# Two-layer feed-forward of a macaron block: the two K halves of the first layer joined in PSUM, all eight groups of the second layer split into high and low parts

## The reference

```
x = x + 0.5 * ffn(layernorm(x))          # ffn: h = LN(x)*gamma + beta; silu(h @ w1 + b1) @ w2 + b2
x = x + attn(layernorm(x))               # sigmoid / tanh gates, a scan over time, output matmul
x = x + 0.5 * ffn(layernorm(x))
w = (q - 128) * scales[k // 128]         # one scale for 128 rows of K and one output column
```

## Time and profile before

| | |
|---|---|
| median of three runs | 780.07 us |
| the profiled execution | 778.86 us |
| its span, first to last instruction | 777.0 us |
| mean granted TensorE clock | 0.985 |
| busy: TensorE, ScalarE, VectorE, GpSimd | 95%, 85%, 82%, 82% of the span |
| first feed-forward, first product of tiles 0, 1, 2, 3 | 15.60, 40.10, 62.33, 82.15 us |
| second feed-forward, first product of tiles 0 and 2 | 462.43, 508.98 us |

### The profile page before, as it was taken

The page is one execution under the profiler, slowest core; times in us unless marked ns, Lnnn a source line. Parts: engine busy times, 40 slices in busy tenths (PEclk is TensorE's granted clock), DMA queues, the critical chain, the costliest instruction groups (busy, mean ns, idle before and its releaser), DMA issues.

```text
span 777.0 us, 14017 instructions
## 1 busy us (share of the span) xinstructions
PE 736.8 (95%) x3262; PEld 549.8 (71%) x3262; DVE 640.0 (82%) x1242; ACT 663.8 (85%) x1123; POOL 636.8 (82%) x821
## 2 busy tenths in 40 slices
PE   5698999999999999999999996989999999999996
PEld 4366777777777776668788783667777777777774
DVE  5377989999999998878778864779899999999886
ACT  5877999999999998778888887779989999999984
POOL 6588999999999987848666676889999999999853
PEclk7989999999999999999999999899999999999999
DMA  8640000000000000000000000000000110000001
GB/s 258 194 135 1 2 0 0 0 0 0 0 0 0 2 0 1 1 1 0 0 0 0 1 1 1 0 29 28 28 27 27 34 48 27 27 27 28 28 28 56
DMA packets 19820, 20.24 MB, mean 26 GB/s; under 512 B 1548, under 2 KB 19394, under 8 KB 19778
## 3 DMA queue, kind: packets, MB, share of 16 engines
q1 hardware_dynamic: 19680, 19.74, 7.8%
q10 hardware_dynamic: 98, 0.02, 0.0%
HBM read 11.37 MB, written 8.39 MB: 25 GB/s over the span
## 4 chain that ended last, share of the span: by engine, by line
PE 84%; issue 5%; POOL 5%; ACT 2%; DVE 2%; DMA 1%; ACTq 0%; DVEq 0%; POOLq 0%
PE ps_fc L867 28%; PE ps_z L867 26%; PE ps_z L901 13%; PE ps_fc L967 7%; PE ps_tr L860 4%; PE ps_tr L917 3%; POOL h_lo L393 2%; PE ps_fc L975 2%; POOL g_lo L403 1%; PE ps_fc L961 1%; DVE z_acc L685 1%; PE ps_z L860 1%; DMA rows<-in_L_attn_bc 1%; POOL xhat L372 1%; ACT xhat L532 0%
## 5 line engine op out<-in xcount | busy, mean ns | idle before, releaser
L685 DVE SCALAR_TENSOR_TENSOR z_acc<-ps_z,cols,z_acc 128x512 f32<-128x512 f32 x384 | 276.7, 742 | 25.2 <-PE ps_z L867 23.7
L403 POOL TENSOR_TENSOR g_lo<-g_full,g_hi 128x512 fp32r<-128x512 f32 x192 | 248.5, 1295 | 49.9 <-ACT g_hi L569 47.5
L547 ACT ACTIVATE u_sb<-ps_fc,cols 128x512 f32<-128x512 f32 x256 | 199.6, 780 | 60.8 <-PE ps_fc L867 54.9
L867 PE MATMUL ps_fc<-h_hi,q_sb 128*128 128x512 f32 x512 | 227.0, 443 | 6.1 <-DVE y_sb L674 3.9
L674 DVE SCALAR_TENSOR_TENSOR y_sb<-ps_fc,cols,u_sb 128x512 f32<-128x512 f32 x256 | 190.3, 743 | 50.5 <-ACT u_sb L547 50.4
L867 PE MATMUL ps_fc<-h_lo,q_sb 128*128 128x512 f32 x512 | 202.9, 396 | 0.0
L867 PE MATMUL ps_z<-g_hi,q_sb 128*128 128x512 f32 x384 | 155.2, 404 | 12.0 <-DVE z_acc L685 11.9
L867 PE MATMUL ps_z<-g_lo,q_sb 128*128 128x512 f32 x384 | 152.3, 397 | 0.0
L567 ACT ACTIVATE g_full<-y_sb 128x512 f32<-128x512 f32 x192 | 120.0, 625 | 9.8 <-DVE y_sb L674 9.8
L867 PEld LDWEIGHTS ps_fc<-h_hi,q_sb 128*128 128x128 f32 x512 | 97.7, 191 | 33.4 <-DVE y_sb L674 7.1
L901 PE MATMUL ps_z<-g_native,w_full 128*128 128x512 f32 x256 | 120.1, 591 | 0.0
(11 more groups left out here) (99 smaller groups left out, 980.5 us busy)
## 6 DMA issues: line engine op xcount, KB each, us to landing
resid<-in_L_attn_x SPq DMA_DIRECT2D x15, 512.0 KB, 4.4
out_x<-resid SPq DMA_DIRECT2D x15, 512.0 KB, 2.9
q_int<-in_L_ffn_fc_q SPq DMA_DIRECT2D x4, 512.0 KB, 7.0
resid<-in_L_attn_x SPq DMA_DIRECT2D x2, 256.0 KB, 3.0
out_x<-resid SPq DMA_DIRECT2D x2, 256.0 KB, 2.3
z_acc<-in_L_ffn_fc_scales SPq DMA_DIRECT2D x1, 256.0 KB, 9.2
wd_sb<-in_L_attn_Wd SPq DMA_DIRECT2D x1, 256.0 KB
wy_raw<-in_L_attn_Wy SPq DMA_DIRECT2D x2, 64.0 KB
```

What stands on the lines that cost most here:

```text
L403: nc.gpsimd.tensor_tensor(g_lo[:, slot, :], g_full[:, g % 2, :], g_hi[:, slot, :].bitcast(F32), ALU.subtract).then_inc(g_ready, 1)
L547: nc.scalar.activation(u_sb[:, f % 2, :], ps_fc1[:, f % 2, 0, :], ACT.Identity, bias=col(R_B1 + f), scale=col(R_S1 + f)).then_inc(u_ready, 1)
L685: nc.vector.scalar_tensor_tensor(out=z, in0=bank_of(g, n, par), scalar=col(R_S2 + KC * g + n), in1=z, op0=ALU.mult, op1=ALU.add).then_inc( ...
L867: last = nc.tensor.matmul(out, w, v, start=start and i == 0, stop=stop and i == len(pairs) - 1)
```

## The change

- First layer: each group has one bank of four, not two. `half_products` computes K half 0 in step f; then one instruction scales the bank in place by s1[0]/s1[1] and adds a bias (`scale_half`: on ScalarE in steps 0, 1, 5, 6, 7, on VectorE in steps 2, 3, 4); in step f + 1 `add_products` accumulates K half 1 on top. The silus read PSUM and take s1[1] as their scale. `u_sb` and `y_sb` are gone.
- beta leaves the tiles: its product with w1 is folded into the bias by small operations at the start. ScalarE now writes `h_hi` from `ps_tr` in one instruction (`round_h`), and VectorE writes `h_lo` from `ps_tr` (`lower_h`). It is `lower_h` that now signals `turned_out`. `h_full` and GpSimd's `h_low` are gone.
- Second layer: all eight groups are split. ScalarE's first sum takes group 0 (steps 4 and 5); VectorE adds seven groups, 14 additions for a tile where there were 12.
- The tables: `add_ffn` moves to steps 6 and 7, the variance to step 6, `lower_h` stands in steps 2 and 4, `round_h` in 1 and 3. The 14 warm-up matmuls go.

```diff
-    NATIVE = 2
-    RSQRT_AT = (5, 3, 2)
-    NORMALISE_AT = ((6, 7), (6, 7), (5, 6))
-    TURN_AT = ((4, 5), (2, 4), (0, 2))
-    ADD_AT = (5, 6)
+    SCALED_ON_ACT = (0, 1, 5, 6, 7)
+    SCALED_ON_DVE = (2, 3, 4)
+    VARIANCE_AT = 6
+    RSQRT_AT = (5, 2, 2)
+    NORMALISE_AT = ((6, 7), (5, 6), (5, 6))
+    TURN_AT = ((3, 5), (1, 3), (0, 2))
+    TURN_OUT_AT = ((4, 6), (2, 4), (1, 3))
+    H_LOWER_AT = ((5, 7), (3, 5), (2, 4))
+    FIRST_SUM_AT = (4, 5)
+    ADD_AT = (6, 7)
...
+            def scale_half(ff, f):
+                act.wait_ge(half_done, FC * ff + (f + 1))
+                nc.scalar.activation(bank, bank, ACT.Identity, bias=bias[:, f:f + 1],
+                                     scale=ratio[:, f:f + 1]).then_inc(scaled_on_act, 1)
...
+            def lower_h(ln, ff, par, c, bank=ps_tr):
+                dve.wait_ge(h_hi_ready, 2 * ff + (c + 1))
+                nc.vector.scalar_tensor_tensor(out=h_lo[:, par, c, :], in0=bank[:, :], scalar=col(R_GAMMA + c),
+                                               in1=h_hi[:, par, c, :].bitcast(F32), op0=ALU.mult,
+                                               op1=ALU.subtract).then_inc(turned_out, 1)
...
                     for f in range(FC):                      # VectorE
+                        if f in SCALED_ON_DVE:
+                            scale_half(ff, f)
                         if before or here:
-                            add_group(*group, range(1))
-                        second_group(FC * ff + f, f)
-                        if before or here:
-                            add_group(*group, range(1, KC))
+                            add_group(ff if here else ff - 1, (f - LAG) % FC, par if here else 1 - par)
+                        if behind and f in H_LOWER_AT[before]:
+                            lower_h(ln + 1, ff + 1, 1 - par, H_LOWER_AT[before].index(f))
...
                     for f in range(FC):                      # TensorE
-                        fc1(FC * ff + f, ff, f, par)
+                        half_products(ff, ln, f, par)
-                            fc2(ff, f - LAG, par)
+                            fc2(*group, 0)
+                            add_products(ff, ln, f - 1, par)
+                            fc2(*group, 1)
```

More of the change, by code:

```diff
@@ L195, in macaron_kernel @@
         fc2_done = sem("fc2_done")
+        z_begun = [sem(f"z{n}_begun") for n in range(KC)]
         z_added = [sem(f"z{n}_added") for n in range(KC)]
@@ L444, in tile @@
                             rsqrt(ln0 + 1, True)
[L445 to L449, removed]
+                        if not before and f == 1:
+                            normalise(ln0 + 1, 1, halves[0])
+                        if ff0 == 0 and not behind and f in XN_LOWER_AT:
+                            xn_low(0, 0, XN_LOWER_AT.index(f))
+                        if behind >= 1 and f == RESIDUAL_AT[before]:
+                            residual(ln + 1, t + 1)
                         if behind >= 2 or ff0 == 0:
@@ L475, in mixer_tile @@
                     rsqrt(t + (NT + 2), behind == 1)
[L476 to L480, removed]
+                for c in range(KC) if behind else ():
+                    xn_low(t + 1, 1 - par, c)
                 if behind == 1:
@@ L833, in mixer_tile @@
                         add_mixer(t - 1, 1 - par, half)
+                for c in range(KC) if not behind else ():
+                    lower_h(2 * NT, NT, 0, c, (ps_tr, ps_tr2)[c])
                 dve.wait_ge(state_ready, t + 1)
@@ L866, in products, with half_products @@
                 for i, (w, v) in enumerate(pairs):
-                    last = nc.tensor.matmul(out, w, v, start=start and i == 0, stop=stop and i == len(pairs) - 1)
+                    last = nc.tensor.matmul(out, w, v, start=start and i == 0, stop=stop and i == len(pairs) - 1,
+                                            skip_group_check=not start)
                 return last
-            def fc1(step, ff, f, par):
+            def half_products(ff, ln, f, par):
                 if f == 0:
-                    pe.wait_ge(h_ready, 2 * ff + 2)
-                wait(pe, y_ready, step - 1)
-                for k in range(KC):
-                    if type(ff) is int and ff == 0 and f == 0:
-                        pe.wait_ge(q1_ready, k + 1)
-                    last = products(ps_fc1[:, f % 2, k, :],
-                                    [(w[:, k, f * P:(f + 1) * P], h[:, par, k, :])
-                                     for w in q1_parts for h in (h_hi, h_lo)])
-                last.then_inc(fc1_done, 1)
@@ L883, in fc2, with add_products @@
-            def fc2(ff, g, par):
-                if native(g):
+                    pe.wait_ge(turned_out, 2 * ln + 1)
+                    if type(ff) is int and ff == 0:
+                        pe.wait_ge(q1_ready, 1)
+                wait(pe, g_hi_ready, FC * ff + (f - 3))
+                products(ps_fc1[:, f % 4, :], [(w[:, 0, f * P:(f + 1) * P], h[:, par, 0, :])
+                                               for w in q1_parts for h in (h_hi, h_lo)]).then_inc(half_done, 1)
+            def add_products(ff, ln, f, par):
+                if f == 0:
+                    pe.wait_ge(turned_out, 2 * ln + 2)
+                    if type(ff) is int and ff == 0:
+                        pe.wait_ge(q1_ready, KC)
+                if f in SCALED_ON_ACT:
+                    pe.wait_ge(scaled_on_act, scaled_count(ff, f, SCALED_ON_ACT))
+                else:
+                    pe.wait_ge(scaled_on_dve, scaled_count(ff, f, SCALED_ON_DVE))
+                products(ps_fc1[:, f % 4, :], [(w[:, 1, f * P:(f + 1) * P], h[:, par, 1, :])
+                                               for w in q1_parts for h in (h_hi, h_lo)],
+                         start=False).then_inc(fc1_done, 1)
@@ new lines, in fc2, with beta_products @@
+                    pe.wait_ge(g_ready, FC * ff + (g + 1))
+                bank = bank_of(g, n, par)
+                wait(pe, *filled_before(BANKS[2 * par + n][g], g, n, ff, par))
+                at = slice(n * P, (n + 1) * P)
+                last = products(bank, [(w[:, g, at], v[:, g % 4, :]) for w in q2_parts for v in (g_hi, g_lo)])
+                last.then_inc(fc2_done, 1)
+            def beta_products(k, q, first=False):
+                for f in range(FC):
+                    last = nc.tensor.matmul(ps_beta_of(k, f), q[:, k, f * P:(f + 1) * P], beta_parts[:, k, :],
+                                            start=first and f == 0, stop=True, skip_group_check=True)
+                return last
@@ L1039, in _ @@
                 pe.wait_ge(wide_ready, KC + 1)
+                pe.wait_ge(bias_ready, 1)
+                for k in range(KC):
+                    last = beta_products(k, q1_low)
+                last.then_inc(beta_low_done, 1)
+                pe.wait_ge(wide_bias_ready, 1)
                 program()
```

334 lines of the change are left out of this document (172 added, 162 removed).

## The result

The changed kernel takes **846.74 us** (median of 4 runs, 845.68 to 848.86) against 780.0 us (779.71 to 782.04), a ratio of 1.085 with a 95% interval of 1.083 to 1.088. It is slower, as forecast, inside the range of 804 to 853, and 17 us slower than the forecast's 830.

A forecast was written before the change was run, and what follows sets the result against it. TensorE, never waiting in steady tiles, was taken as the bound. Less matmul work plus three added waits made steady tiles longer (+32.8 and +32.5 us by stage); with 2 x -7.2 for first tiles, +50.9: 830 us, range 804 to 853.

The forecast's parts named there:

- Removed from TensorE: Two native groups become split groups: 1.56 us less in a tile, 16.66 us for a steady tile without waits.
- Wait a: TensorE's second turn in step 2 waits for VectorE's lower_h, listed behind both additions of group 6: 1.76 us.
- Wait b: turn_back of half 1 in step 6 waits for add_ffn, behind two additions and the variance on VectorE: 2.05 us.
- Wait c: In step 5, group 1's second product pair waits for the bank that ScalarE's first sum empties: 0.34 us.
- They add: The three added waits of a tile sum, as each is a round trip starting from TensorE's own last product.
- A steady tile: TensorE's reduced work plus the three added waits: 20.8 us against 18.22 before.
- The first two tiles: Tiles 0 and 1 of each stage gain as idle time and slow products go: net -7.2 us for a stage.
- The start: Small operations on beta at the start, no warm-up: between 1 us less and 2 more, taken as 0.
- R1: Rival: the added waits cost nothing and GpSimd is next, 758 us; chance 0.06.
- its ring: Closed chain from xhat's second half through turn, silu, g_lo and GpSimd's list to the next xhat: 18.5 us a tile.
- R2: Rival: only one of the two waits for VectorE at the turns is real, 777 or 769 us; chance 0.05.
- R3: Rival: TensorE's clock falls too after two stops in every tile, adding 94 us: 924 us; chance 0.06.

The follow-up runs named there:

- no_a: The changed kernel with lower_h ahead of the two additions in its VectorE step: 815.3 us (one run).
- var_behind: The changed kernel with add_ffn ahead of the variance in VectorE's step 6: 840.0 us.
- no_b: The changed kernel with add_ffn back in VectorE's steps 5 and 6: 796.8 us (one run).
- before_var: The kernel before with only the variance moved a step later, to step 6: 775.2 us.
- no_ab: The changed kernel with add_ffn back in VectorE's steps 5 and 6 and lower_h ahead of the additions: 772.9 us.
- before_b: The kernel before with only add_ffn moved from VectorE's steps 5 and 6 to 6 and 7: 895.7 us (one run).

## Why the prediction was right, point by point

- **Removed from TensorE, right.** A tile without its waits is 20.96 - 1.87 - 1.92 - 0.43 = 16.74 us (the waits from the points below, each as a delay of TensorE's next start, which is 0.1 to 0.3 more than the idle time in the view), forecast 16.66.
- **Wait a, right.** Forecast 1.76; the turn at 279.64 comes 2.15 after the product at 277.49, less 0.24 is 1.91 (in the other of the loop's two tiles 1.83). Its parts: 1.27 to the start of `h_lo` (forecast 1.21), 0.88 from there to TensorE (0.79). One part was read too simply. The forecast lets the last product release the second addition. In wait b it does, 0.44 us after its start; in wait a that addition starts 0.61 after it, because VectorE is still in a row of its own, the scaling (276.73) and the first addition (277.44). So nearly 0.2 us of wait a is VectorE's own queue. The run no_a gave back 31 us and not the 61 of its theory, because ScalarE's `h_hi` and GpSimd's `g_lo` are late next; the forecast priced no such next wait for a.
- **Wait b, right.** Forecast 2.05; measured 2.20 - 0.24 = 1.96 (1.88). Parts: 1.11 to the variance (1.21), 0.29 for it (0.34, and var_behind confirms it), 0.80 for `add_ffn` and the way back (0.74). The errors in the parts cancel in a and b together: 3.81 forecast, 3.79 measured.
- **Wait c.** 0.16 us of idle in the view, but the pair comes 0.43 later in all: at 243.62 it stands 0.56 after the product ahead, then 0.34, instead of twice 0.23. Forecast 0.34, inside its ends. In the first tiles the idle time is 0.73 or 0.74 us, which no term had.
- **They add, right.** no_b removes b and leaves a's 50.6 us as it was; no_a leaves b's 52.1.
- **A steady tile, right.** 20.96 against 20.8. From the first `turn_back` of tile 2 on, the two stages took 4.3 us more than the forecast had, which is this 0.16 us in 28 tiles.
- **The first two tiles, wrong; it is the step that failed.** "Net -7.2 for a stage." From the first product of tile 0 to that of tile 2 the first stage took 46.10 us instead of 46.73, and the second 47.01 (496.55 to 543.56) instead of 46.55: 0.2 us won in both together, where 14.4 were booked. By the first `turn_back` of tile 2, 76.67 us in the trace against 77.55, the first stage had won 0.9 us; the second, from the last `turn_back` of the first stage on, 0.6 (557.93 - 366.25 against 524.22 - 331.99; of that, the mixer up to the second stage's first product is unchanged, 130.30 against 130.44). That is 13.0 of the 17.3 us by which the span, 68.2 longer, exceeds the +50.9. The stops above 0.3 us of tiles 0 and 1 in the timeline after, all on TensorE:

```profile
25.01 0.66 PE L894 MATMUL ps_tr<-ident,xhat 128*128 128x128 f32 x4 [2.98 <-POOL xhat L372]
29.67 0.50 PE L901 MATMUL ps_z<-g_hi,q_sb 128*128 128x512 f32 x1 [0.74 <-ACT z_acc L553]
32.00 0.63 PE L894 MATMUL ps_tr<-ident,xhat 128*128 128x128 f32 x4 [1.59 <-DVE h_lo L673]
41.20 0.66 PE L894 MATMUL ps_tr<-ident,xhat 128*128 128x128 f32 x4 [1.11 <-POOL xhat L372]
47.35 0.63 PE L894 MATMUL ps_tr<-ident,xhat 128*128 128x128 f32 x4 [1.76 <-DVE h_lo L673]
51.97 0.50 PE L901 MATMUL ps_z<-g_hi,q_sb 128*128 128x512 f32 x1 [0.73 <-ACT z_acc L553]
54.30 1.09 PE L958 MATMUL ps_tr<-ident,z_acc 128*128 128x128 f32 x4 [1.59 <-DVE h_lo L673]
59.97 0.63 PE L958 MATMUL ps_tr<-ident,z_acc 128*128 128x128 f32 x4 [1.81 <-DVE resid L695]
```

  The stop of 5.45 us is gone and so is VectorE's of 8.39, as forecast. But these eight sum to 12.3 us where the forecast booked 7.3. Missed were the two waits for `xhat` (4.1 us, booked as 1), the first `turn_back` of tile 1, which in that tile's own table waits for `lower_h` (1.59, in no term), and c at double its size. TensorE's busy time fell by 3.5 us, where 4.7 were booked for slow products and native groups. before_var shows a like thing in the old kernel: taking away the longest stop of a start-up handed most of its time to the next ones.
- **The start.** The first product comes at 16.20 instead of 15.60: 0.6 us, inside the forecast's -1 to +2.
- **Rivals.** R1's premise fell (the waits are there), but its ring is real: 18.5 forecast, 18.8 in no_ab once the waits were out, and 772.9 us. It had 758 for the total, partly because it counted the same gain in the first tiles, 12.8 us for a stage. R2 fell, both a and b are real. R3 fell for this kernel: the steady window is at 1.00. Its own terms, 60 x 8 x 0.2, make 96 us and not 94.

## What to carry to other kernels

Where TensorE's list has an instruction that waits for VectorE, look at what VectorE's own list has ahead of that signal: if an operation there needs TensorE's latest product, the chain is a stop. Its parts from the trace predicted each stop here to within 0.15 us, as long as every part was counted; in before_b two were not, and the time was 63 us off. Here such an order cost more than the arithmetic that the change saves. The same arithmetic with both signalling operations listed first gave 772.9 instead of 846.7 us, and with GpSimd's and ScalarE's lists put in order too 739.9. Do not book the idle time of a start-up as a gain when its longest stop goes, and price what is late next for each wait that you remove.

## What the hardware showed beyond the forecast

In the steady tiles the clock held through the stops of the change, and in before_b it did not. Twice in each tile the change stops TensorE for 1.67 to 1.81 us, and the steady window reads a granted clock of 1.00, the upper of the two levels (2.4 GHz). The run before_b stops it for 2.40 and 0.69 us, and its window reads less:

```profile
80.00:310.00 230.00, 199.90 (x820) 145.14 (x819) 170.41 (x322) 170.61 (x287) 176.44 (x227) 0.95 0.00 0
```

After seven of its eleven long stops in this window four to eight products come about 0.43 us apart instead of 0.23. In the stretch below, 308.10 to 311.50, the granted clock reads 0.56, close to the lower level (1.2 GHz):

```profile
308.12 1.09 PE L917 MATMUL ps_tr<-ident,z_acc 128*128 128x128 f32 x4 [2.38 <-DVE resid L693]
308.86 0.78 PE L867 MATMUL ps_fc<-h_hi,q_sb 128*128 128x512 f32 x1
309.43 0.63 PE L867 MATMUL ps_fc<-h_lo,q_sb 128*128 128x512 f32 x1
309.86 0.63 PE L867 MATMUL ps_fc<-h_hi,q_sb 128*128 128x512 f32 x1
```

After the stop of equal length at 264.02 they did not (1.00 from 264.00 to 268.00), and after one of 1.59 us in tile 1 of the changed kernel (54.30) they did (0.53 from 54.30 to 57.50). So the length of a stop alone does not decide, and no run here isolates what does. The Trainium skill ("TensorE: Matmul & The Clock Gate", section on psum-queue depth-cycling) describes a kernel that cycles through PSUM banks and whose TensorE stands idle briefly between groups, often enough that the clock swings between its two levels. before_b bears that out with 0.95, the steady tiles of the change do not.
